# Six edits of order at both ends of a transformer block: early queries, low parts, bias passes, an own bank, whole splits, shared sums

## The reference

```python
def _attn(xq, ctx, wq, wkv, wo, bo):
    q = _heads(xq @ wq)
    k, v = jnp.split(ctx @ wkv, 2, axis=-1)
    ...
    q = _rope(q, sq, cq)
    k = _rope(k, sk, ck)
    sim = jnp.einsum('bhnd,bhmd->bhnm', q, k) * DH ** (-0.5)
    a = jax.nn.softmax(sim, axis=-1)
    ...
    return o @ wo + bo
attn_in = _adaln(x, cond, ln1_w, ln1_b, g1_w, g1_b, b1_w, b1_b)
x = _attn(attn_in, attn_in, sa_wq, sa_wkv, sa_wo, sa_bo) + x
cross_in = _adaln(x, cond, ln1_w, ln1_b, g1_w, g1_b, b1_w, b1_b)
ctx_n = _ln(context, ca_lnc_w, ca_lnc_b)
x = _attn(cross_in, ctx_n, ca_wq, ca_wkv, ca_wo, ca_bo) + x
ffn_in = _adaln(x, cond, ln2_w, ln2_b, g2_w, g2_b, b2_w, b2_b)
h = jax.nn.gelu(ffn_in @ ff_w1 + ff_b1, approximate=False)
x = h @ ff_w2 + ff_b2 + x
```

## Time and profile before

| | us |
|---|---|
| median of 3 runs | 1115.08 |
| lowest and highest | 1114.47, 1115.96 |
| the profiled execution | 1118.88 |
| its span, first to last instruction | 1117.1 |
| PE busy in the span | 1097.2 (98%) |
| DVE busy | 858.1 (77%) |
| POOL busy | 775.7 (69%) |
| ACT busy | 636.9 (57%) |

### The profile page before, as it was taken

One profiled execution on the slowest core, in us unless ns is written; L12 is line 12 of the kernel. 1 busy time (PEld: TensorE's weight loads), 2 busy tenths in 40 slices (PEclk: granted clock), 3 DMA queues, 4 the chain that ended last, 5 costly groups with the idle time before them and its releaser, 6 DMA issues.

```text
span 1117.1 us, 18312 instructions
## 1 busy us (share of the span) xinstructions
PE 1097.2 (98%) x6904; PEld 785.1 (70%) x6904; DVE 858.1 (77%) x1023; ACT 636.9 (57%) x895; POOL 775.7 (69%) x503
## 2 busy tenths in 40 slices
PE   8989999999999999999999999999999999989998
PEld 7657666776666776666766667766666776756997
DVE  5878887878787777878888777777877777788554
ACT  6465565665666555577665555555555545775521
POOL 2687887787788767789799766777777667755210
PEclk9899999999999999999999999999999999999999
DMA  6312121311231111211121112211121111300001
GB/s 175 86 46 57 32 53 39 89 30 30 53 77 38 39 36 23 72 39 39 29 63 38 39 39 59 51 23 36 38 72 39 37 31 30 114 1 1 20 19 38
DMA packets 59606, 52.31 MB, mean 47 GB/s; under 512 B 23040, under 2 KB 42496, under 8 KB 59264
## 3 DMA queue, kind: packets, MB, share of 16 engines
q1 hardware_dynamic: 57632, 49.57, 18.5%
q10 hardware_dynamic: 1888, 1.59, 0.5%
HBM read 15.22 MB, written 2.10 MB: 16 GB/s over the span
## 4 chain that ended last, share of the span: by engine, by line
PE 90%; DVE 5%; ACT 2%; issue 1%; DMA 1%; SPq 0%; POOL 0%; ACTq 0%; POOLq 0%; DVEq 0%
PE ps L872 18%; PE ps L713 12%; PE ps L715 11%; PE ps L714 11%; PE ps L813 6%; PE ps L860 6%; PE ps L848 5%; PE ps L819 5%; PE ps L815 5%; PE ps L817 5%; PE ps L963 4%; DVE lo L1083 1%; PE ps L729 1%; DMA x<-x_dram 1%; DVE w_lo L1117 1%
## 5 line engine op out<-in xcount | busy, mean ns | idle before, releaser
L548 ACT ACTIVATE probs<-ps 128x1024 f32<-128x1024 f32 x256 | 262.5, 1027 | 208.0 <-PE ps L819 183.6
L1065 DVE TENSOR_REDUCE neg_max<-ps 128x2 f32<-128x1024 f32 x256 | 301.6, 1226 | 76.7 <-PE ps L848 76.7
L420 POOL TENSOR_TENSOR acc<-acc,probs 128x1024 f32<-128x1024 f32 x128 | 306.2, 2392 | 18.6 <-POOL acc L415 0.4
L872 PE MATMUL ps<-probs,v 128*64 128x512 f32 x1024 | 230.7, 592 | 0.0
L415 POOL TENSOR_TENSOR acc<-probs 128x1024 f32<-128x1024 f32 x64 | 153.2, 2394 | 72.1 <-ACT probs L548 72.1
L872 PEld LDWEIGHTS ps<-probs,v 128*64 128x64 f32 x1024 | 73.9, 137 | 146.1 <-issue 146.1
L429 POOL TENSOR_TENSOR eo<-tmp 128x512 f32<-128x512 f32 x63 | 89.7, 1424 | 120.2 <-DVE tmp L1092 120.1
L1092 DVE TENSOR_TENSOR tmp<-ps,rope 128x1024 f32<-128x1024 f32 x126 | 148.2, 1211 | 4.5 <-PE ps L715 4.3
L813 PE MATMUL ps<-max_rows,pick 64*128 64x512 f32 x512 | 109.3, 419 | 2.6 <-DVE o_lo L1079 1.6
L713 PE MATMUL ps<-xn_hi,w_hi 128*128 128x512 f32 x256 | 107.8, 421 | 2.5 <-DVE o_lo L1079 1.3
L848 PE MATMUL ps<-hi 64*128 64x512 f32 x512 | 104.8, 400 | 5.4 <-DVE neg_max L1065 2.6
(11 more groups left out here) (116 smaller groups left out, 2250.0 us busy)
## 6 DMA issues: line engine op xcount, KB each, us to landing
lo<-eo SPq DMA_DIRECT2D x126, 256.0 KB, 3.2
w_raw<-pack_dram SPq DMA_DIRECT2D x16, 192.0 KB, 3.9
x<-x_dram SPq DMA_DIRECT2D x4, 512.0 KB, 7.5
w_raw<-pack_dram SPq DMA_DIRECT2D x8, 256.0 KB, 4.3
max_rows<-neg_max SPq DMA_DIRECT2D x128, 2.0 KB, 2.0
w_raw<-w_dram SPq DMA_DIRECT2D x2, 1024.0 KB, 5.8
out<-x SPq DMA_DIRECT2D x8, 256.0 KB, 2.2
ctx_in<-ctx_dram SPq DMA_DIRECT2D x4, 384.0 KB, 4.2
```

Source lines behind the costliest of these rows:

```text
L420: pool.tensor_tensor(acc[:, g % 2, :, :], acc[:, g % 2, :, :], probs[:, i, :, :], ALU.add).then_inc(added, 1)
L548: act.activation(probs[:, i, :, :], score_ps(i), ACT.Exp, scale=SCALE).then_inc(exped, 1)
L872: mm = pe.matmul(av_ps[DH * h:DH * h + DH, :], v[:, u % 2, kt, c:c + DH], probs[:, kt, h, :], start=(kt == 0), stop=(kt == TT - 1))
L1065: dve.tensor_reduce(neg_max[:, g % 2, :, i], peak_ps(i), AX.X, ALU.max, negate=True).then_inc(maxed, 1)
```

## The change

It has six parts.

1. The queries of the second quad (job 3, 12 matmuls) stood behind both transposes of the third norm. They now stand between and behind the four maxima of pair 0 (`project_3`).
2. The low parts of pair 1 were VectorE's, at the start of its period 0. They are now GpSimd's, ahead of rotate(2), and have a semaphore of their own. ScalarE makes the high parts of pair 1 ahead of the guess for the third norm, not behind it.
3. The four bias passes of self-attention are GpSimd's in periods 13, 15, 18 and 21 and no longer in 0, 1, 5 and 7. They wait for the sum of the last self-attention quad of their batch row (`o_added`), and `add_out` no longer waits for them in the first eight quads.
4. The averages of pair 61 go to bank 5. score(62) no longer waits for the copy of the averages and for the low parts of the output; peak(63, 0) does.
5. VectorE splits each of the two MLP matrices in one instruction of 2048 elements. The first split stands ahead of normalise(61), it stood behind low_o(61). In period 61 the statistics stand ahead of normalise(60) and their means ahead of low_o(60).
6. Of the last pair's sums GpSimd makes one pass instead of three. VectorE adds blocks 2 and 3 (`add_last_probs`), and `total(63)` has four matmuls instead of two.

The diff, without the two new semaphores' lines:

```diff
@@ -126,7 +126,9 @@
-        av_ps = ps[:, 1, :]
+        def av_ps(g):
+            return ps[:, 5 if g == PAIRS - 3 else 1, :]
         ada_ps = (ps[:, 0, :], ps[:, 1, :])
@@ -234,7 +238,7 @@
         bias_in = {at[0] + 3: n for n, at in norm_at.items() if n >= NB and at[1] is not None and order[n][0] == X}
-        bias_in.update({0: 0, 1: 1, 5: 2, 7: 3})
+        bias_in.update({13: 0, 15: 1, 18: 2, 21: 3})
@@ -434,6 +438,8 @@
                 pool.wait_ge(ln_rows, TT * (n + 1))
+                if sublayer == 0:
+                    pool.wait_ge(o_added, 2 * (NB + b) + 2)
                 pool.tensor_tensor(x[:, b, :, :], x[:, b, :, :],
@@ -444,8 +450,9 @@
                     add_probs(p, 1)
-                    add_probs(p, 2)
-                    add_probs(p, 3)
+                    if p < PAIRS - 1:
+                        add_probs(p, 2)
+                        add_probs(p, 3)
                 if p in stats_in:
@@ -463,6 +470,8 @@
             refine_rstd(pool, 2)
+            pool.wait_ge(qk_high, 2)
+            pool.tensor_tensor(lo[:, 1, :, :], raw_qk[:, 1, :, :], hi[:, 1, :, :], ALU.subtract).then_inc(qk_low_1, 1)
             rotate(2)
@@ -565,7 +574,7 @@
                     act.wait_ge(o_ready, g)
-                act.copy(av[:, :], av_ps).then_inc(av_kept, 1)
+                act.copy(av[:, :], av_ps(g)).then_inc(av_kept, 1)
@@ -646,8 +655,8 @@
             high_qk(0)
+            high_qk(1)
             guess_rstd(2)
-            high_qk(1)
             norm_rows(2)
@@ -740,14 +749,25 @@
                 for e in range(2):
-                    if j in (1, 3):
-                        pe.wait_ge(roped, 2 * (j - 1) + e + 1)
-                    if j == 3 and e == 1:
-                        pe.wait_ge(maxed, 3)
+                    if j == 1:
+                        pe.wait_ge(roped, e + 1)
                     for kt in range(KT):
...
                                    a_hi[0:rows, b, kt, :], a_lo[0:rows, b, kt, :], kt == 0, kt == KT - 1)
+                    mm.then_inc(projected, 1)
+            def project_3(e, kt):
+                if e == 0 and kt == 0:
+                    pe.wait_ge(w_split, 2)
+                    pe.wait_ge(ln_split, 4)
+                if e == 1 and kt == 0:
+                    pe.wait_ge(maxed, 3)
+                c = slice(kt * 256 + e * 128, kt * 256 + (e + 1) * 128)
+                mm = parts(job_ps(3, e), w_hi[:, 0, c], w_lo[:, 0, c], xn_hi[:, 1, kt, :], xn_lo[:, 1, kt, :],
+                           kt == 0, kt == 1)
+                if kt == 1:
                     mm.then_inc(projected, 1)
@@ -794,11 +814,14 @@
                 if kt == 0:
-                    pe.wait_ge(qk_low, g + 1)
+                    if g == 1:
+                        pe.wait_ge(qk_low_1, 1)
+                    else:
+                        pe.wait_ge(qk_low, max(g, 1))
                     pe.wait_ge(max_landed, 32 * (g + 1))
-                    if g > 0:
+                    if g > 0 and g != PAIRS - 2:
                         pe.wait_ge(av_kept, g)
-                    if g > 1:
+                    if g > 1 and g != PAIRS - 2:
                         pe.wait_ge(o_low, g - 1)
@@ -835,6 +858,7 @@
                         pe.wait_ge(o_low, PAIRS - 3)
+                        pe.wait_ge(av_kept, PAIRS - 2)
                     if g == 1 and i == 1:
@@ -849,15 +873,19 @@
             def total(g):
-                pe.wait_ge(added, 3 * g + 3)
+                pe.wait_ge(added, 3 * g + (3 if g < PAIRS - 1 else 1))
                 if g == PAIRS - 4:
...
                     pe.wait_ge(o_added, 2 * (QUADS - 1))
+                    pe.wait_ge(last_added, 1)
                 for h in range(2):
-                    mm = pe.matmul(sum_ps(g)[DH * h:DH * h + DH, :], ones[:, :], acc[:, g % 2, h, :], start=True, stop=True)
+                    out = sum_ps(g)[DH * h:DH * h + DH, :]
+                    mm = pe.matmul(out, ones[:, :], acc[:, g % 2, h, :], start=True, stop=g < PAIRS - 1)
+                    if g == PAIRS - 1:
+                        mm = pe.matmul(out, ones[:, :], tmp[:, 0, h, :], start=False, stop=True)
                 mm.then_inc(summed, 1)
@@ -869,7 +897,7 @@
                     c = a * 128 + h * DH
-                    mm = pe.matmul(av_ps[DH * h:DH * h + DH, :], v[:, u % 2, kt, c:c + DH], probs[:, kt, h, :],
+                    mm = pe.matmul(av_ps(g)[DH * h:DH * h + DH, :], v[:, u % 2, kt, c:c + DH], probs[:, kt, h, :],
                                    start=(kt == 0), stop=(kt == TT - 1))
@@ -923,11 +951,14 @@
             modulate(3)
+            project_3(0, 0)
             peak(0, 2)
+            project_3(0, 1)
             peak(0, 3)
+            project_3(1, 0)
+            project_3(1, 1)
             norm(2, 0)
             norm(2, 1)
-            project(3)
             for p in range(PAIRS):
@@ -979,7 +1010,7 @@
                 if b == 0:
-                    pe.wait_ge(ffw_split, 8)
+                    pe.wait_ge(ffw_split, 2)
                     blocks(0, 1)
@@ -1003,7 +1034,7 @@
-            pe.wait_ge(ffw_split, 4)
+            pe.wait_ge(ffw_split, 1)
             pe.wait_ge(o_added, 2 * (QUADS - 1))
@@ -1101,7 +1132,7 @@
                 _, b, phase = quad(u)
-                if r == 0:
+                if r == 0 and u >= 2 * NB:
                     dve.wait_ge(biased, NB * phase + b + 1)
@@ -1109,34 +1140,34 @@
-            def split_ffw(m, c):
-                cut = slice(c * N, (c + 1) * N)
-                dve.wait_ge(ffw_high, 4 * m + c + 1)
+            def split_ffw(m):
+                dve.wait_ge(ffw_high, 4 * m + 4)
                 high, low, raw = ((w1_hi, w1_lo, w1_raw), (w2_hi, w2_lo, w2_raw))[m]
-                flat = [t.rearrange("p k f -> p (k f)") for t in (high, low, raw)]
-                dve.tensor_tensor(flat[1][:, cut], flat[2][:, cut], flat[0][:, cut], ALU.subtract)\
-                   .then_inc(ffw_split, 1)
+                dve.tensor_tensor(low[:, :, :], raw[:, :, :], high[:, :, :], ALU.subtract).then_inc(ffw_split, 1)
+            def add_last_probs():
+                dve.wait_ge(exped, 4 * PAIRS)
+                dve.tensor_tensor(tmp[:, 0, :, :], probs[:, 2, :, :], probs[:, 3, :, :], ALU.add).then_inc(last_added, 1)
...
                         peak(p + 1, i)
-                if p == 0:
-                    low_qk(1)
+                if p == PAIRS - 3:
+                    norm_stats(stats_in[p])
+                if p == PAIRS - 2:
+                    split_ffw(0)
                 if is_pair(p - 1):
                     normalise(p - 1)
-                if p in stats_in and p != PAIRS - 3:
-                    norm_stats(stats_in[p])
+                if p == PAIRS - 1:
+                    add_last_probs()
+                if p in stats_in:
+                    if p != PAIRS - 3:
+                        norm_stats(stats_in[p])
                     norm_means(stats_in[p])
...
                     low_o(p - 1)
-                if p == PAIRS - 3:
-                    norm_stats(stats_in[p])
-                    norm_means(stats_in[p])
-                if p == PAIRS - 2:
-                    for c in range(4):
-                        split_ffw(0, c)
                 if is_pair(p + 2) and p not in stats_in:
@@ -1148,8 +1179,7 @@
                 if p == PAIRS - 2:
-                    for c in range(4):
-                        split_ffw(1, c)
+                    split_ffw(1)
```

More of the change, by code:

```diff
@@ L179, in build @@
         qk_low = sem("qk_low")
+        qk_low_1 = sem("qk_low_1")
         peaked = sem("peaked")
@@ L187, in build @@
         added = sem("added")
+        last_added = sem("last_added")
         averaged = sem("averaged")
```

## The result

The changed kernel takes **1120.59 us** (median of 6, 1120.05 to 1121.16); the kernel before, run beside it, 1115.52 (6 runs, 1114.47 to 1118.14). The ratio is 1.0045, 95% interval 1.0032 to 1.0057: slower by 5.1 us, outside the range of 1111.0 to 1117.5. The two profiled executions differ by far less: 1120.12 us against 1118.88, spans 1118.3 against 1117.1. Most of the question is in the middle one.

What follows compares the result with a forecast made beforehand. TensorE holds 90% of the chain, so time counts only where it stands or runs at half clock. Start -1.4, biases +1.4 and tail -0.1 sum to -0.1 us: median 1115.08 to 1115.0, range 1111.0 to 1117.5.

Steps and rivals of the forecast that it cites:

- The base: Whole kernel: sum made on the profiled 1118.88 us, the median taken 3.8 below it, so 1115.08 goes to 1115.0.
- Step 1: Start: maxima land later, score(0,0) starts near 45.4 after a 7 us stand; total(0) ends 1.4 us sooner.
- Step 2: Moved biases: period 18's bias goes ahead of low_qk(20), a wait before period 19's first maximum, +1.4 us.
- Step 3: Periods 61 to 63: split_ffw(0) delays o_lo of pair 61, TensorE stands 3.6 us; gains behind it leave -0.1 us.
- Rival (d): Start and tail: half clock lasts some 6.8 us, not 3.9, after the stands; +3.0, 1118.1 us; chance 0.16.
- The rule weighed: split_ffw(0) beside GpSimd: exclusive lock ends it at 999.1; slowdown at 1000.6, sum 1.5 us more, 1116.5.
- (a): Period 62: VectorE has the first turn, the clock holds; -3.6 there instead of -0.1, 1111.5 us; chance 0.16.
- (b): Period 18: VectorE has the first turn, the +1.4 falls away, 1113.6 us; chance 0.13.
- (c): Start: maxima land in 1.9 us, clock back within 2; -3.3, 1113.1 us; chance 0.14.

Runs made afterwards that it cites:

- e16: The kernel before, unchanged, run again for its profile; the profiled execution took 1115.80 us.
- e5: The kernel before, unchanged, run a third time for its profile; the profiled execution took 1113.98 us.
- e11: The kernel before with only the change to project(3), high_qk(1) and the low parts of pair 1: 1117.67 us, ratio 1.0020.
- e12: The kernel before with only the biases moved to periods 13, 15, 18 and 21, with their two waits: 1115.70 us, ratio 0.9997.
- e13: The changed kernel with 14 matmuls that nobody reads in TensorE's stand ahead of project_out(30): 1117.86 us, ratio 1.0012.
- e7: The kernel before with only the change to periods 61 to 63 (bank, order, splits, last sums): 1118.88 us, ratio 1.0030.
- e10: The changed kernel with split_ffw(0) behind low_o(61), biases in periods 13, 15, 21 and 23, and 24 unread matmuls ahead of score(0,0): 1112.77 us.
- e6: The kernel before with unread matmuls in TensorE's waits: 6 ahead of peak(2,0), 2 ahead of total(63), 5 ahead of hidden(1): 1115.57 us, ratio 0.9997.
- e15: Kernel before, its start kept, with biases in 13, 15, 21, 23, the change's tail but split_ffw(0) behind low_o(61), and unread matmuls ahead of norm(2,0), peak(2,0): 1111.29 us.
- e4: The changed kernel with only split_ffw(0), in one piece, back behind low_o(61) on VectorE: 1114.45 us, ratio 0.9977.
- e1: The kernel before, unchanged, run once more; the profiled execution took 1118.61 us.

## Why the prediction was wrong, step by step

**The base.** The sum was made against the profiled execution, and then: "the median lies 3.8 below it, so 1115.08 goes to 1115.0". This step failed first, and it is the largest part of the miss: 3.4 of the 5.2 us between the forecast -0.1 and the measured +5.1. I saw the 3.8 us and carried them over as if they lay outside the kernel, though that execution's span is 1117.1, so only 1.8 us lie outside it, as in every other execution of this kernel within 0.3. They lay for the most part at 63 and at 1019, in stretches of half clock from which two of my gains came: at total(0), "at full clock it takes 0.9 instead of 1.8", and behind hidden(1), "falls away, 1.7 us". Against e16 the first cost 1.6 (I had priced it at 1.9) with 0.6 more in period 3, the second 1.2; against e5 there is also 1.3 at 36. If the heaps are told by the stretch at 63, some two thirds of the executions don't have it, and the one at 1019 stood in one profile of four. The Trainium skill (TensorE: Matmul & The Clock Gate, Part 1) says that the number of slow matmuls at a kernel's start differs from run to run of one kernel. In the four profiles the half clock differs too, at 36 (0.50 to 0.72 over six microseconds) and in mid-kernel, at 63 and 1019.

Between the two profiled executions, for which the sum was made, the terms came out at -2.6 for the start (-1.4 forecast), +1.6 for the biases (+1.4), +2.3 for the end (-0.1) and -0.1 for the periods between: +1.2 in place of -0.1. That this is within 1.4 us of the forecast is luck, as the first and the third term are each off and in opposite directions.

**Step 1, the start.** The path was right: rotate(2) ends at 40.4 (40.6 forecast), score(0,0) starts at 45.21 (45.4), the stand is 6.68 us (7). One turn was not: low_qk(0) started at 37.25 and not at 36.79, so GpSimd's first pass of rotate(2) went ahead of it (1.28 us) and the second waited (2.24), with the same end. Then score(2,0) is 2.0 us sooner than in the profile of before, and 3.0 is gained at period 8 (forecast -1.4, bounds to -3.5). Against the two profiles of the lower heap it is +0.5 and -0.5 there. The stand (4.3 to 6.7 us) brought the clock down in every profile that has this start with its stand unfilled, while what it replaces did so at 63 in two profiles of four. In this number two edits of opposite sign are hidden, which I had put into one term. Against e5, project(3) and the low parts alone cost 2.5 us at period 4 (e11), and the bias out of period 0 gives 2.3 (e12).

**Step 2, the biases.** Right: period 18's bias had its turn first (330.98), low_qk(20) took 3.32 us (3 forecast), and the step ahead of period 20 is 1.5 us (1.4). The short wait that was to move from behind period 6 to behind 14 gave 0.4 at score(8,0) and cost 0.5 at score(16,0).

**Step 3, the tail.** Forecast -0.1, measured +2.3 between the profiles and +3.5 against e5 (6.88 - 2.64 up to score(63,0), less 0.8 behind it) and against e16. The order of events was right: GpSimd's sum ahead, split_ffw(0) for 4.28 us (4.1), a stand of 3.62 (3.6). Two terms were mis-sized. project_out(30) started 1.84 us later in its period, not 1.4. And the clock: I took 3.9 us of it, of which "0.6 is under ScalarE's own queue", 1.3 us. It was down from about 1001 to 1007.7 (0.66, 0.50 and 0.71 in the three stretches above), the whole of project_out(30), and cost 2.4 us (e13), with nothing hidden; in e7 it cost 1.3. Rival (d), which lets it last 6.8 us, was the nearest to what happened, for this stand and not for the one at the start.

**The rule weighed.** GpSimd's sum from 994.03 was over at 996.4, and split_ffw(0) ended at 998.55, 2.15 us behind it, which is about a full-length pass (the second split, with no neighbour, took 2.28), while GpSimd's next sum, 2.4 us elsewhere, shows 4.21:

```profile
996.54 4.21 POOL L424 TENSOR_TENSOR acc<-acc,probs 128x1024 f32<-128x1024 f32 x1
```

So each waited for the whole of the other. A slowdown would have ended the split at 1000.6. The rows agree with the exclusive lock of the Trainium skill (SBUF — State Buffer, the part on the shared port pair). They also show what is wrong with the edit: a long piece takes its turn once, but whatever stands behind it waits for all of it.

**Rivals (a), (b), (c).** In neither place did VectorE have the first turn. (c) has the number of the profile (-3.0 for its -3.3), but neither of its conditions held: the maxima landed as late as forecast, and the clock was back 3.4 us after TensorE resumed, not 2. In the medians even the number is absent.

## What to carry to other kernels

Before a prediction rests on a stretch of half clock, ask whether the profiled execution is the usual one: where its time is above the median, the excess may be in the trace, and a gain taken from it will not show in the median. A second and a third profile of the unchanged kernel tell: here two of one heap differed by 1.8 us. A long stand of TensorE costs its length and then a stretch at half clock behind it; matmuls that nobody reads held the clock up in e13 (2.4 us in the trace) and in some executions of e10; in e6 they did not take the upper heap away, and in e15 not the half clock at 36. And a long two-operand VectorE instruction belongs behind the small ones that TensorE waits for, not ahead of them (6.1 us in e4).

## What the runs showed of the hardware

- In a stand of 3.62 us the granted clock fell to 0.50 about 1 us before TensorE resumed, and stayed there for 5.7 us after in the changed kernel and for 2.9 in e7. In one of 6.68 us it was at 0.50 from 42 to 45 and was back 3.4 us after TensorE resumed. After waits of 1.3 to 1.7 us with work between them it fell in some executions of one kernel and not in others.
- Executions of one kernel pace the steady periods differently. From score(36,0) to score(61,0) it is 378.7 or 378.8 us in the profiles of before (1118.88), e5 and after, 379.5 in e7 and e16, and 380.0 in e1, at a granted clock of 1.00 and with TensorE busy for all of 600 to 900 us. That is up to 1.2 us over 25 periods. The cause is open.
